# Attention, maxima and feed-forward shares in two 64-row tiles of TensorE, and a new way to load the stacks

## The reference

```
qkv    = xn @ w_qkv                              # 16 heads of 16
q, k   = irfft(rfft(q) * sigmoid(mask_logits)), the same for k      # along the 16 of a head
attn   = softmax(q k^T / 4) v, over 2048 keys, then @ w_out + b_out
h      = square(relu(xn @ W_fc^T))               # 256 -> 1024
y      = h @ W_proj^T                            # 1024 -> 256
5 times: mem = 0.9 mem + y - (mem > 1); spk = mem > 1;  the branch is mean(spk)
```

## Time and profile before

| | us |
|---|---|
| median of 3 runs (lowest, highest) | 1822.28 (1821.86, 1823.49) |
| the profiled execution | 1822.3 |
| its span, first to last instruction | 1820.4 |
| TensorE busy (matmuls) | 1807.8 |
| VectorE busy | 1423.1 |
| ScalarE busy | 1075.5 |
| GpSimd busy | 711.7 |

### The profile page before, as it was taken

One profiled execution on the slowest core, in us unless ns is written; L12 is line 12 of the kernel. 1 busy time (PEld: TensorE's weight loads), 2 busy tenths in 40 slices (PEclk: granted clock), 3 DMA queues, 4 the chain that ended last, 5 costly groups with the idle time before them and its releaser, 6 DMA issues.

```text
span 1820.4 us, 35332 instructions
## 1 busy us (share of the span) xinstructions
PE 1807.8 (99%) x14308; PEld 1088.7 (60%) x14308; DVE 1423.1 (78%) x1782; ACT 1075.5 (59%) x1182; POOL 711.7 (39%) x948
## 2 busy tenths in 40 slices
PE   8999999999999999999999999999999999999999
PEld 5665555556555556555555666555566665555666
DVE  6787787778777877887788778777877787788766
ACT  3336666666666666666666666666666666666662
POOL 1003333444433344444333444433344444333445
PEclk9999999999999999999999999999999999999999
DMA  5652022222211222222112222210222222112223
GB/s 175 225 211 48 20 39 45 43 45 41 43 29 25 44 44 44 45 39 44 21 34 44 43 45 45 39 36 18 45 45 43 45 39 44 25 30 45 44 79 113
DMA packets 86495, 98.82 MB, mean 54 GB/s; under 512 B 51062, under 2 KB 65142, under 8 KB 82490
## 3 DMA queue, kind: packets, MB, share of 16 engines
q1 hardware_dynamic: 83164, 93.42, 23.3%
q10 hardware_dynamic: 3168, 3.15, 0.6%
HBM read 70.80 MB, written 20.99 MB: 50 GB/s over the span
## 4 chain that ended last, share of the span: by engine, by line
PE 97%; DVE 2%; DMA 1%; issue 0%; ACT 0%; ACTq 0%; SPq 0%
PE ring L679 32%; PE banks L689 28%; PE ring L669 18%; PE banks L751 6%; PE banks L756 6%; PE banks L624 2%; PE ring L835 2%; PE ring L671 1%; PE ring L636 1%; PE ring L615 1%; DMA attnT<-x 0%; DVE pmax L912 0%; DVE attnT L883 0%; PE ring L592 0%; DVE counts L906 0%
## 5 line engine op out<-in xcount | busy, mean ns | idle before, releaser
L917 DVE TENSOR_REDUCE pmax<-ring 128x2 f32<-128x1024 f32 x1000 | 1176.7, 1218 | 325.1 <-PE ring L671 322.4
L548 ACT ACTIVATE probs<-ring 128x1024 f32<-128x1024 f32 x1024 | 993.5, 1022 | 634.2 <-PE ring L679 632.9
L679 PE MATMUL ring<-qst,kst 66*128 66x512 f32 x2048 | 613.4, 421 | 0.7 <-DVE pmax L917 0.4
L689 PE MATMUL banks<-probs,vst 128*32 128x256 f32 x8192 | 548.2, 385 | 0.1
L679 PEld LDWEIGHTS ring<-qst,kst 66*128 66x128 f32 x2048 | 344.4, 188 | 257.8 <-issue 209.1
L669 PE MATMUL ring<-kst,qst 64*128 64x512 f32 x1000 | 386.9, 466 | 0.0
L671 PE MATMUL ring<-kup,qup 64*128 64x512 f32 x1000 | 386.3, 466 | 0.0
L689 PEld LDWEIGHTS banks<-probs,vst 128*32 128x32 f32 x8192 | 213.7, 109 | 213.1 <-issue 124.4
L460 POOL TENSOR_TENSOR lif<-lif 128x256 f32<-128x256 f32 x32 | 21.7, 677 | 793.4 <-ACT y_sb L564 793.4
L669 PEld LDWEIGHTS ring<-kst,qst 64*128 64x128 f32 x1000 | 182.8, 183 | 158.9 <-DVE pmax L917 82.2
L671 PEld LDWEIGHTS ring<-kup,qup 64*128 64x128 f32 x1000 | 182.7, 183 | 0.0
(11 more groups left out here) (76 smaller groups left out, 686.3 us busy)
## 6 DMA issues: line engine op xcount, KB each, us to landing
qup<-qk_scratch SPq DMA_DIRECT2D x252, 64.0 KB, 3.5
qst<-qk_scratch SPq DMA_DIRECT2D x120, 128.0 KB, 4.0
kst<-qk_scratch SPq DMA_DIRECT2D x60, 256.0 KB, 6.0
qk_scratch<-attnT SPq DMA_DIRECT2D x32, 256.0 KB
kup<-qk_scratch SPq DMA_DIRECT2D x62, 128.0 KB, 6.4
qk_scratch<-probs SPq DMA_DIRECT2D x16, 256.0 KB
qst<-shiftT SPq DMA_DIRECT2D x256, 2.0 KB
attnT<-o_turned SPq DMA_DIRECT2D x256, 16.0 KB, 1.9
```

Source lines behind the costliest of these rows:

```text
L548: act.activation(probs[:, s % PS, :], score_slot(g), ACT.Exp, scale=SCALE).then_inc(exp_done, 1)
L679: mm = pe.matmul(score_slot(g)[:, c * BLK:(c + 1) * BLK], kst[b][:, kt * P:(kt + 1) * P], qst[b][:, q:q + BLK], start=True, stop=True)
L689: mm = pe.matmul(po[32 * j:32 * (j + 1), half * D:(half + 1) * D], vst[b][:, kt, :], quarters[:, j], start=(kt == 0), stop=(kt == TB - 1))
L917: dve.tensor_reduce(pmax[:, tile, 2 * part:2 * part + 2], unit_slot(g).rearrange("p (c e) -> p c e", c=2), AX, ALU.max).then_inc(mx_taken, 1)
```

## The change

- **Two tiles of 64 rows.** `kst` and `qst` have 128 rows: the 64 rows of products twice, for a lower and an upper tile (`rows_of`). `qup` and `kup` are gone. A unit of scores is two matmuls at once, columns 0 to 511 on the lower tile and 512 to 1023 on the upper, and then two `shifted` matmuls at once that add the shift: weights `ones`, moving `shift_rows`, in which only two rows of each tile hold the shift. The maxima of the even unit run on the lower tile with the upper half of the share between them, those of the odd unit on the upper tile with the lower half of the share (`up` and `down` with a side). In the last head's steps without maxima the shares go between the scores. Even and odd unit of a pair use one slot, one after the other.
- **Maxima.** VectorE reduces the first 512 columns of the even unit (`even_max`); ScalarE copies the other 512 to SBUF (`take_half`), and VectorE reduces them there (`even_half`); the odd unit is reduced as before. ScalarE copies before the two exponentials of the pair.
- **VectorE's other work** (`beside_maxima`) stands after the even maximum, and an output half is spread over several pairs.
- **Stack in halves.** `load_stack` loads 1024 keys and queries with five DMAs: the keys in one, from a source of 4 copies x 32 rows, the queries in four, each from a source of 2 copies x 16 rows. Each half has its semaphore; step 8 waits for the first, step 16 for the second. The shift is stored with eight DMAs, four for each tile. SyncE stores the shift before it moves the output.
- **Filter.** The front multiplies a real Fourier matrix by its gates (one instruction of VectorE) and forms the filter in one matmul (`make_filter`); the fold follows the first transposes. ScalarE issues the loads of logits and matrix. The first 48 maxima use all 128 rows, so they come out double, and VectorE halves them (`halve`). The scratch tensor of zeros is gone.

The diff, cut to what the text speaks of (the removed functions stand in full above):

```diff
-ROWS = 4 * DH + 2
...
-PIECE = 6 * 16
 USES = 3
-STACK = 6 * 16
+STACK = 5 * 16
+SHIFT = 8 * 16
...
-        qst = [sb(f"qst{i}", [ROWS, S], F32R) for i in range(2)]
-        kst = [sb(f"kst{i}", [ROWS, S], F32R) for i in range(2)]
-        qup = sb("qup", [P, S], F32R)
-        kup = [sb(f"kup{i}", [P, HALF], F32R) for i in range(2)]
+        qst = [sb(f"qst{i}", [P, S], F32R) for i in range(2)]
+        kst = [sb(f"kst{i}", [P, S], F32R) for i in range(2)]
+        shift_rows = sb("shift_rows", [P, S], F32R)
+        ones = sb("ones", [P, P], F32R)
...
+            return ring[:, (4 * (g // 2) + 1 + g % 2) % 3, :]
+        def unit_slot(g):
+            return ring[:, (4 * (g // 2) + 3 * (g % 2)) % 3, :]
...
+            def load_stack(h, b, piece):
+                cols = slice(piece * HALF, (piece + 1) * HALF)
+                tok = slice(b * S + piece * HALF, b * S + (piece + 1) * HALF)
+                keys = qk_dram[1:2, h, :, :, tok].rearrange("a r d t -> a (r d) t").broadcast_to([4, 2 * DH, HALF])
+                sp.dma_start(kst[b][:, cols].bitcast(F32), keys).then_inc(stack_in[b][piece], 16)
+                for side in range(2):
+                    for part in range(2):
+                        r = side * SIDE + part * 2 * DH
+                        queries = qk_dram[0, h, part:part + 1, :, tok].broadcast_to([2, DH, HALF])
+                        sp.dma_start(qst[b][r:r + 2 * DH, cols].bitcast(F32), queries).then_inc(stack_in[b][piece], 16)
...
+            def store_shift(n, half):
                 sp.wait_ge(shift_turned, n + 1)
                 cols = slice(half * HALF, (half + 1) * HALF)
...
+                for side in range(2):
+                    dst = shift_rows[side * SIDE:side * SIDE + 2, cols].rearrange("r (t j q) -> r t j q", j=4, q=32)
+                    for j in range(4):
+                        sp.dma_start(dst[:, :, j, :].bitcast(F32), shiftT[32 * j:32 * j + 16, :]).then_inc(shift_in, 16)
...
+                if t in (2, 4):
+                    wait_stored(t // 2)
+                    load_stack(0, 0, t // 2 - 1)
...
+                    load_stack(h + b, 1 - b, 0)
+                    load_stack(h + b, 1 - b, 1)
+                store_shift(2 * i + 1, 1)
...
+            def take_half(p):
+                act.wait_ge(half_ready, p + 1)
+                act.wait_ge(half_max, p)
+                act.activation(half_sb[:], unit_slot(2 * p)[:, BLK:2 * BLK], ACT.Copy).then_inc(half_taken, 1)
...
+            def make_filter():
+                pe.wait_ge(filt_dve, 3)
+                pe.matmul(odd_slot[:, 0:P], dft_sb, gated_sb, start=True, stop=True).then_inc(filter_done, 1)
...
+            def rows_of(side):
+                return slice(side * SIDE, (side + 1) * SIDE)
+            def maximum(g, s, b, c, side):
+                (tile, part), rows = unit_of(s), rows_of(side)
+                key = (2 * part + c) * BLK
+                return pe.matmul(unit_slot(g)[:, c * BLK:(c + 1) * BLK], qst[b][rows, tile * P:(tile + 1) * P],
+                                 kst[b][rows, key:key + BLK], start=True, stop=True)
+            def scores(g, s, b, side, c):
                 half, kt = s // TB, s % TB
...
+                q = half * HALF + c * BLK
+                pe.matmul(score_slot(g)[:, c * BLK:(c + 1) * BLK], kst[b][rows_of(side), kt * P:(kt + 1) * P],
+                          qst[b][rows_of(side), q:q + BLK], start=True, stop=False)
+            def shifted(g, s, side, c):
+                q = s // TB * HALF + c * BLK
+                mm = pe.matmul(score_slot(g)[:, c * BLK:(c + 1) * BLK], ones[rows_of(side), :],
+                               shift_rows[rows_of(side), q:q + BLK], start=False, stop=True)
+                if c == 1:
+                    mm.then_inc(score_ready, 1)
...
+                even, odd = s % STEPS, (s + 1) % STEPS
+                if ahead:
+                    if g:
+                        pe.wait_ge(exp_done, g + 1)
+                    if s == LEAD:
+                        pe.wait_ge(stack_in[mb][0], STACK * (h + 1 + b))
+                    if s == LEAD + TB // 2:
+                        pe.wait_ge(stack_in[mb][1], STACK * (h + 1 + b))
+                    maximum(g, s, mb, 0, 0).then_inc(mx_ready, 1)
+                    if share:
+                        share(1, 0)
+                    maximum(g, s, mb, 1, 0 if share else 1).then_inc(half_ready, 1)
+                    if share:
+                        share(1, 1)
                 if scored:
                     if s % STEPS == 0:
...
+                        pe.wait_ge(shift_in, SHIFT * (2 * i + (3 if s else 1)))
                     if s == TB:
...
+                        pe.wait_ge(shift_in, SHIFT * (2 * i + 2))
+                    score_free(g)
+                if scored and (ahead or not share):
+                    scores(g, even, sb_, 0, 0)
+                    scores(g, even, sb_, 1, 1)
+                    shifted(g, even, 0, 0)
+                    shifted(g, even, 1, 1)
+                    score_free(g + 1)
+                    scores(g + 1, odd, sb_, 0, 0)
+                    scores(g + 1, odd, sb_, 1, 1)
+                    shifted(g + 1, odd, 0, 0)
+                    shifted(g + 1, odd, 1, 1)
+                elif scored:
+                    scores(g, even, sb_, 0, 0)
+                    share(1, 0)
+                    scores(g, even, sb_, 0, 1)
+                    share(1, 1)
+                    shifted(g, even, 0, 0)
+                    score_free(g + 1)
+                    scores(g + 1, odd, sb_, 1, 0)
+                    shifted(g, even, 0, 1)
+                    scores(g + 1, odd, sb_, 1, 1)
+                    share(0, 0)
+                    shifted(g + 1, odd, 1, 0)
+                    share(0, 1)
+                    shifted(g + 1, odd, 1, 1)
+                if between:
+                    between()
                 if ahead:
...
+                    if share:
+                        share(0, 0)
+                    pe.wait_ge(mx_taken, taken(g))
+                    maximum(g + 1, s + 1, mb, 0, 1 if share else 0)
+                    if share:
+                        share(0, 1)
+                    pe.wait_ge(half_taken, g // 2 + 1)
+                    maximum(g + 1, s + 1, mb, 1, 1).then_inc(mx_ready, 1)
...
+            def up(tile, f, side, c):
+                return pe.matmul(misc[:, (f % 4) * P:(f % 4 + 1) * P], wfc_sb[rows_of(side), c, f * P:(f + 1) * P],
+                                 xnT[rows_of(side), c, tile * P:(tile + 1) * P],
+                                 start=(side == 1 and c == 0), stop=(side == 0 and c == KC - 1))
+            def down(f, side):
+                return pe.matmul(misc[:, 0:D], hid_sb[rows_of(side), f, :], wproj_sb[rows_of(side), f, :],
+                                 start=(f == 0 and side == 1), stop=(f == FC - 1 and side == 0))
...
+            def even_max(g, s):
+                tile, part = unit_of(s)
+                dve.wait_ge(mx_ready, FIRST_MAX + g + 1)
+                dve.tensor_reduce(pmax[:, tile, 2 * part:2 * part + 1], unit_slot(g)[:, 0:BLK], AX,
+                                  ALU.max).then_inc(mx_taken, 1)
+            def even_half(g, s):
+                tile, part = unit_of(s)
+                dve.wait_ge(half_taken, g // 2 + 1)
+                dve.tensor_reduce(pmax[:, tile, 2 * part + 1:2 * part + 2], half_sb[:], AX, ALU.max).then_inc(half_max, 1)
...
+            def beside_maxima(h, b, s, last):
+                i = 2 * h + b
+                g = STEPS * i + s
+                if s == FIRST and i:
+                    scale_output(2 * i - 1)
+                if s == LEAD:
+                    for link in range(4):
+                        split_shift(link, 2 * i + 1, 1, FIRST_MAX + g)
+                if s == LEAD + 4 and i:
+                    turn_output(2 * i - 1)
+                if s == TB + LAG:
+                    take_output(h, b, 0)
+                if s == TB + LAG + 2:
+                    weigh_output(2 * i)
+                if s == TB + LAG + 4:
+                    scale_output(2 * i)
+                if s == LEAD + TB and not last:
+                    for link in range(4):
+                        split_shift(link, 2 * i + 2, 0, FIRST_MAX + g)
+                if s == LEAD + TB + 4:
+                    turn_output(2 * i)
+                if s == STEPS + LAG:
+                    take_output(h, b, 1)
+                if s == STEPS + LAG + 2:
+                    weigh_output(2 * i + 1)
...
+                for s in range(FIRST, STEPS + FIRST, 2):
+                    g = STEPS * (2 * h + b) + s
                     if s < LEAD or not last:
...
+                        even_max(g, s)
```

More of the change, by code:

```diff
@@ L564, in head @@
                         act.activation(y_sb[:], misc[:, 0:D], ACT.Copy).then_inc(misc_taken, 1)
-                    if s == 34 and not last:
+                    if s == 33 and not last:
                         take_up(i + 1, 0, UP_A)
```

(12 more changed lines are left out.)

450 lines of the change are left out of this document (167 added, 283 removed).

## The result

The changed kernel takes 2101.4 us (median of 4 runs, 2098.5 to 2107.0) against 1822.3: ratio 1.153, 95% interval 1.152 to 1.155. The forecast was 2046, in a range of 1920 to 2190. All ratios here are to the kernel before, run on the same chip.

What follows compares the result with a forecast made beforehand. TensorE, busy 99%, bounds the kernel before; after the change the stack loads on few DMA engines decide. 1822.3 + 32 (front) + 192 (thirty heads) = 2046 us; forecast's own range 1960 to 2140, full range 1920 to 2190.

Steps and rivals of the forecast that it cites:

- Loads on few engines: Stack loads: keys run on 4 DMA engines, queries on 2 of those, at 25.5 GB/s each; 15.4 us a half.
- The carrying over: Stack loads: engine count follows a source's outermost dimension (4 or 2), though the trace showed it only for destinations.
- Times of landing: Each head, from its first maximum: first half in at 16.4 us, second 31.9, shift about 33.5; head 58.8 against 52.4.
- TensorE in program order: Odd maxima wait behind the share, 0.11 or 0.22 us late: up pairs take 3.16 us, down pairs 3.27.
- the prediction's first estimate, 3.05: TensorE's pair of steps with one change of tiling less, before any delay from program order: 3.05 us against 3.26.
- Rival 1: Stack loads spread over 16 engines or two separate sets, so nothing waits: 1788 us, down to 1706; chance 0.14.
- Rival 2: Granted clock falls in each head's two stalls, 2 us each: 120 us over 30 heads, 2166 us; chance 0.11.
- Rival 3: Row tiles don't hide weight loads: beats 0.10 us longer, pair 4.0, 2236 us or more; chance 0.05.
- VectorE and ScalarE "fit": Per pair: VectorE's work is 2.9 of 3.2 us; ScalarE's is 2.54 us plus three small copies a head.
- three small copies a head: ScalarE: extra work named beside its 2.54 us a pair, given no size of its own.
- The front and head 0: Before and in head 0: 20 us TensorE wait before block 6; head 0 ends at 205 us, not 172.4; +32.
- The end: Last head: few maxima and no loads, so no change: 0.

Runs made afterwards that it cites:

- Experiment 1: Changed kernel with every copy of keys and queries in the stack loaded by a DMA of its own: 1733.8 us, ratio 0.951.
- experiment 4: Kernel before the change, with only its query loads (qst and qup) taken from sources of 2 copies: 2196.7 us, ratio 1.205.
- experiment 8: Second half of the stack issued three pairs later: changed kernel 2117.8 us, ratio 1.162; changed kernel with queries loaded copy by copy 1799.6 us, ratio 0.987.
- experiment 5: On top of Experiment 1, the odd unit's first maximum placed ahead of both records of the share: 1730.3 us, ratio 0.950.
- Experiment 9: On top of Experiment 1, VectorE's shift chain split over two pairs and the last head's output preparation moved later: 1716.6 us, ratio 0.942.
- Experiments 9 and 10: Experiment 9, and on top of it (10) ScalarE's relu cut from 512 to 64 columns: 1699.7 us, ratio 0.932.
- experiment 7: Changed kernel with 30 extra matmuls on TensorE just ahead of step 8's wait for the first half of the stack: 2111.2 us, ratio 1.158.

## Why the prediction was right, step by step

- **Loads on few engines: right, and it decides.** Four engines, then two, at 22.5 and 26 GB/s where 25.5 was taken. Experiment 1 turns 2101 into 1734, experiment 4 brings the harm into the old kernel. The carrying over from a destination's dimension to a source's, which no row of before showed, holds: 22 closing packets are 4 for each load of keys and 2 for each of queries. By the Trainium skill ("DMA: Bandwidth & Descriptors", "Why a DMA increments its semaphore by 16 and not by 1") it is 4 and 2 engines too; the trace agrees.
- **Times of landing: sizes off, and this is most of what the forecast missed.** After the first issue the first half had landed at 18.7 in the mean of 30 heads, the second at 33.95, the shift at 35.4. The forecast, counted the same way, had 16.2, 31.7 and 33.3. The second half and the shift took as long as forecast behind what stood ahead of them (15.2 for 15.5, 1.4 for 1.6); the first half is late by 2.5, and everything behind it with it. Its first packet starts 1.4 after the issue, not 0.8, and from there to the landing an engine moves 22.7 GB/s, not 25.5. So the wait at step 8 is 6.6, not 4. That its queries lost time to the second half's loads is not shown: experiment 8 takes nothing off. Behind the shift a head takes 24.6 us (24.0 at the full clock) where the forecast had 25.5. Together a head is 60.0 against 58.8: some 37 us over 30 heads, of the 55 missed.
- **TensorE in program order: wrong.** Pairs are 3.03, near the prediction's first estimate, 3.05; the tiles take matmuls past each other (rows of experiment 5), so the sentence on the kernel before that all engines are in order does not hold for TensorE's two tiles. The Trainium skill ("TensorE: Matmul & The Clock Gate", "The mechanism") has matmuls start and end strictly in program order; the rows of experiment 5 differ (1089.87 ahead of 1089.91), and the measurement decides. Its "TensorEngine Tiling (Array Packing)", "Key Properties", lets different tiles work in parallel, and the trace agrees. The error cost the forecast little, because the pairs ahead of step 16 are not what a head waits for; only the eight after it count, where it is most of the 1.5 us by which 24.0 is shorter than 25.5, and hides part of the late landing. That is luck.
- **Rival 1** had the mechanism wrong and the price nearly right: with loads on 16 engines it gave 1788, or 1706 if the tiles pass each other; measured 1734. Experiments 9 and 10 name two costs that it left out, the end's wait (17.8) and ScalarE's two long pairs (17); that is 35, where 1734 lies 28 above 1706.
- **Rival 2, the clock: it does fall, and costs a seventh of the 120 us.** The lower level follows each first stall, but filling the stall gave no time back (experiment 7). Behind the second stall it falls in 11 of 29 heads and takes 1.5 us each, 17 us in all. In the kernel before with the slow loads, where a single wait decides, 3.2 us a head are lost behind it (experiment 4).
- **Rival 3** did not come: row tiles hide their weight loads, beats are 0.23.
- **VectorE and ScalarE "fit": nearly.** VectorE does; ScalarE's "three small copies a head" were two of 0.60 that don't fit in a pair with 2.54, 0.26 late each. I had averaged them over 16 pairs.
- **The front and head 0: right.** +32 forecast, +31.5 measured; 19.1 us of idle TensorE before block 6 for 20.
- **The end: missed.** Forecast 0; measured +23.2, 7.6 of it the last head that loads. In the last head VectorE stands for x at step 12 and TensorE for VectorE (12.9 in the changed kernel, L649 on `o_sb`). Experiment 9 removes it.

## What to carry to other kernels

A saved instruction in SyncE's queue can cost the kernel its transfers. Where rows are loaded in several copies, give each copy a DMA of its own: the loads with one DMA over several copies cost 367 us here (experiment 1). A single DMA whose outermost dimension is the rows was not tried. Read the DMA share beside the GB/s (0.13 and 0.25 of 16 engines are two and four of them). A stall that is filled shows nothing where a second wait stands behind it: look for what comes next before the stall is priced. And read more heads than one: the head shown first here had the longest wait of all, and beside it a delayed load looked like a gain. Work that comes twice a head has to fit into its own pair; an average over sixteen hides it.

## What the runs showed of the hardware

- Matmuls on two 64-row tiles start independently: one later in the program starts ahead of one on the other tile (1089.87 and 1089.91, 1090.13).
- A DMA engine's rate depends on company: 23.5 (experiment 4) to 26 GB/s with two at work, 18 to 26 with four, 10.8 with thirteen. What sets it within these ranges stays open.
- The lower level of the granted clock outlasts the stall that brought it: TensorE works again from 1066.42, and over 1070 to 1078, without an idle moment, the clock is still 0.84 in the mean.
- The same two short waits (for the second half and for the shift) are followed by a full clock in 18 heads and by a lower one in 11.
